# A perceiver block on one core: an entry norm, a PV product and a softmax placed elsewhere in the ramp of a hand-ordered kernel

## The reference, cut to what matters

```python
x = x + fake_quant(layernorm(x)) @ fake_quant(ctx)      # x (16,64,1024), ctx (16,1024,1024)
qkv = layernorm(x) @ Wqkv                               # 32 heads of 32, one key/value head
p = softmax(where(causal, q @ k.T * scale + alibi, -1e30))
x = x + (p @ v) @ Wo
h = layernorm(x); r = softmax(h @ gate_w.T)             # 8 experts
x = x + (h * (r @ in_scale)) @ sign(W).T * (r @ out_scale) + bias
```

## Time and profile before

| what | us |
|---|---|
| median of 3 runs | 449.78 (448.64 to 451.35) |
| the profiled execution, its own time | 451.25 |
| its span, first to last instruction | 449.5 |
| TensorE busy | 375.2 (83%) |
| VectorE busy | 310.6 (69%) |
| ScalarE busy | 259.3 (58%) |
| GpSimd busy | 97.0 (22%) |

### The profile page before, as it was taken

The page is one execution under the profiler, slowest core; times in us unless marked ns, Lnnn a source line. Parts: engine busy times, 40 slices in busy tenths (PEclk is TensorE's granted clock), DMA queues, the critical chain, the costliest instruction groups (busy, mean ns, idle before and its releaser), DMA issues.

```text
span 449.5 us, 9600 instructions
## 1 busy us (share of the span) xinstructions
PE 375.2 (83%) x3952; PEld 256.8 (57%) x3952; DVE 310.6 (69%) x586; ACT 259.3 (58%) x308; POOL 97.0 (22%) x116
## 2 busy tenths in 40 slices
PE   0445864996999979999999999998999899889565
PEld 0115834963645945596559655964588458745332
DVE  7678479884656858885888588849785975394331
ACT  4777897848495646665657575747565622241110
POOL 5210010001403404140313032312231212021202
PEclk9955996996999999999999999999999999999759
DMA  7999997699588744776477646874491010001001
GB/s 314 383 408 409 409 358 280 210 388 344 196 337 294 231 176 148 268 255 201 140 253 265 211 142 220 296 214 140 167 335 43 0 48 2 3 1 48 0 0 47
DMA packets 30097, 91.97 MB, mean 205 GB/s; under 512 B 8224, under 2 KB 8224, under 8 KB 30048
## 3 DMA queue, kind: packets, MB, share of 16 engines
q1 hardware_dynamic: 27888, 83.40, 52.3%
q10 hardware_dynamic: 2160, 7.87, 4.7%
HBM read 85.50 MB, written 4.19 MB: 200 GB/s over the span
## 4 chain that ended last, share of the span: by engine, by line
PE 60%; DVE 16%; DMA 9%; issue 6%; ACT 6%; POOL 1%; SPq 1%; POOLq 0%; DVEq 0%; ACTq 0%
PE R L1507 10%; DMA ring<-ctx 7%; PE T L1330 7%; PE R L1281 6%; PE R L1283 6%; PE R L1282 6%; PE R L1369 4%; PE R L1372 4%; PE R L1371 4%; PE C L1311 4%; ACT b L522 4%; PE T L1463 3%; DMA aT<-a 2%; DVE Pr L979 2%; DVE st L875 1%
## 5 line engine op out<-in xcount | busy, mean ns | idle before, releaser
L522 ACT ACTIVATE b<-ring,quant,qpar 128x2048 uint8<-128x2048 f32 x64 | 133.0, 2090 | 12.5 <-DMA ring<-ctx 12.0
L1369 PE MATMUL R<-T_hi,Wqkv_hi 128*128 128x128 f16 x448 | 79.3, 223 | 0.0
L1371 PE MATMUL R<-T_lo,Wqkv_hi 128*128 128x128 f16 x448 | 79.2, 222 | 0.0
L1372 PE MATMUL R<-T_hi,Wqkv_lo 128*128 128x128 f16 x448 | 79.2, 222 | 0.0
L1507 PE MATMUL R<-sgn,XS_hi 128*128 128x512 fp8e4 x128 | 49.7, 388 | 0.0
L1507 PE MATMUL R<-sgn,XS_lo 128*128 128x512 fp8e4 x128 | 49.5, 387 | 0.0
L1311 PE MATMUL C<-b,aT 128*64 128x512 f16 x256 | 36.6, 415 | 14.2 <-ACT b L522 10.1
L1369 PEld LDWEIGHTS R<-T_hi,Wqkv_hi 128*128 128x128 f16 x448 | 45.1, 101 | 0.4
L1371 PEld LDWEIGHTS R<-T_lo,Wqkv_hi 128*128 128x128 f16 x448 | 44.6, 100 | 0.1
L1372 PEld LDWEIGHTS R<-T_hi,Wqkv_lo 128*128 128x128 f16 x448 | 44.6, 100 | 0.0
L316 POOL TENSOR_TENSOR Pr<-Pr,mx 128x512 f32<-128x512 f32 x16 | 16.7, 1042 | 127.1 <-DVE mx L984 127.1
(11 more groups left out here) (143 smaller groups left out, 883.5 us busy)
## 6 DMA issues: line engine op xcount, KB each, us to landing
ring<-ctx SPq DMA_DIRECT2D x64, 1024.0 KB, 6.0
ring<-L_attn_Wo SPq DMA_DIRECT2D x4, 1024.0 KB, 7.1
ring<-L_ffn_weight SPq DMA_DIRECT2D x4, 1024.0 KB, 4.9
out<-X ACTq DMA_DIRECT2D x8, 512.0 KB, 2.6
Wo<-L_attn_Wqkv SPq DMA_DIRECT2D x7, 544.0 KB, 15.4
X<-x ACTq DMA_DIRECT2D x7, 512.0 KB, 4.1
sgn<-L_attn_Wqkv SPq DMA_DIRECT2D x1, 544.0 KB, 18.3
X<-x SPq DMA_DIRECT2D x1, 512.0 KB, 12.7
```

The costliest lines, as they stand in the source:

```text
L522: e.activation(b8[:, c % BRING, :], ring[:, slot, :], ACT.Identity, scale=qR2, bias=qZ2).then_inc(s_rf[slot], 1)
L1369: e.matmul(dst, hi, rows[0], start=k == 0 and g == 0, stop=False, skip_group_check=True)
L1371: e.matmul(dst, hi, rows[1], start=False, stop=False, skip_group_check=True)
L1372: last = e.matmul(dst, lo, rows[0], start=False, stop=k == KT - 1, skip_group_check=True)
```

## The change

It writes another order for the ramp. (1) In step 0, the last two k blocks of the second query half come after the transposition of the keys, and ScalarE and VectorE take the key parts between the two query halves. (2) In step 1, the second half of tile 0's probabilities is transposed and multiplied by v around tile 1's second norm: TensorE before and after `t1`, ScalarE and VectorE accordingly; VectorE's row normalization of tile 0 comes after v instead of before the norm. (3) Tile 1's exponentials are taken with one conversion between them, where two and one stood before; the second projection half is cut in two around a transposition; context pair 1 of tile 2 goes behind the router. (4) Tile 3's load, statistics and entry norm go from step 2 into step 1, the norm between the last `attn_rows` and `router_max`; its scratch is XL. SyncE's transposing DMA for tile 3 then stands before two loads of tile 3's context. GpSimd's list follows. The end of `step_1` also changes: `x2(ahead, 1)` before `x1(ahead)`, `context(2, 3)` after the projection, `t1(ahead)` after `ffn(ahead, 1, low)`.

```diff
 turns()
-    uses += of(1, "T10 T11") + of(0, "PT10 PT11 Ta0") + of(1, "Tk") + of(0, "Ta1")
+    uses += of(0, "PT10 PT11") + of(1, "T10 T11") + of(0, "Ta0") + of(1, "Tk") + of(0, "Ta1")
 SyncE
-                if s.is_step(2):
-                    turn_over(2)
+                if s.is_step(2, 3):
+                    turn_over(s.i)
...
-                if s.i > 2:
+                if s.i > 3:
                     turn_over(s.i)
 GpSimd, step_1
+                inv_std(0, 3)
                 inv_std(2, 0)
                 with_row_sum(2)
                 with_bias(0)
+                with_row_sum(3)
+                inv_std(2, 1)
                 inv_std(1, 2)
-                inv_std(2, 1)
 ScalarE, step_1
                 load_x(2)
+                load_x(3)
                 wo_hi(0)
+                pt_hi(s, 1, 0)
+                pt_hi(s, 1, 1)
                 wo_hi(1)
...
+                exp(ahead, 0, 0)
                 conv(2, 0)
-                conv(2, 1)
-                exp(ahead, 0, 0)
-                conv(2, 2)
                 exp(ahead, 0, 1)
...
-                conv(2, 3)
+                conv(2, 1)
...
+                conv(2, 2)
+                conv(2, 3)
+                router_exp(s)
+                ta_hi(ahead, 1)
                 conv(2, 4)
-                router_exp(s)
+                rt_copy(s)
 VectorE
-            def norm0(t, between=lambda: None):
-                if t > 1:
-                    e.wait_ge(s_Ta, (t - 1) * 2)
-                if t == 3:
-                    e.wait_ge(s_T1, 6)
+            def norm0(t, rows, between=lambda: None):
+                if rows is XL:
+                    e.wait_ge(s_T2, (t - 2) * 2)
+                else:
+                    at_least(e, s_Ta, (t - 1) * 2)
...
                 pt_lo(ahead, 0, 1)
+                stats0(3)
                 x2(s, 1)
...
                 attn_rows(ahead, 1, 1)
+                norm0(3, XL)
                 router_max(s)
 TensorE, step_0 and step_1
-                    query(s, 1, [k])
+                    if k < KT - 2:
+                        query(s, 1, [k])
                 tk(s)
+                query(s, 1, range(KT - 2, KT))
...
-                t1(s)
-                kv(s)
                 pt(s, 1, 0)
                 pt(s, 1, 1)
+                t1(s)
+                pv(s, 1, 0)
+                pv(s, 1, 1)
+                kv(s)
                 query(s, 1, low)
                 ta(s, 0)
-                pv(s, 1, 0)
-                pv(s, 1, 1)
...
                 pt(ahead, 0, 0)
+                project(s, 1, high[:2])
                 pt(ahead, 0, 1)
-                project(s, 1, high)
+                project(s, 1, high[2:])
...
                 context(2, 0, s)
-                context(2, 1)
...
                 router_t(s)
-                context(2, 2)
+                context(2, 1)
                 inscale(s, 0)
                 inscale(s, 1)
+                context(2, 2)
                 project(ahead, 0, high)
-                context(2, 3)
                 project(ahead, 1, high)
+                context(2, 3)
```

More of the change, by code:

```diff
@@ L490, in second_half @@
                     inv_std(1, s.i)
-                if s.next:
+                if s.next and not s.is_step(2):
                     inv_std(0, s.i + 1)
@@ L678, in step_0 @@
                 q_hi(s, 0)
+                k_hi(s)
                 q_hi(s, 1)
-                k_hi(s)
                 v_copy(s)
@@ L701, in step_1 @@
                 v_copy(s)
-                pt_hi(s, 1, 0)
-                pt_hi(s, 1, 1)
                 wo_hi(3)
@@ L728, in step_1 @@
                 t2_copy(s, 1)
+                conv(2, 2)
+                conv(2, 3)
+                router_exp(s)
+                ta_hi(ahead, 1)
                 conv(2, 4)
-                router_exp(s)
+                rt_copy(s)
                 conv(2, 5)
-                ta_hi(ahead, 1)
-                rt_copy(s)
+                xs_hi(s, 0)
+                xs_hi(s, 1)
                 conv(2, 6)
                 conv(2, 7)
-                xs_hi(s, 0)
-                xs_hi(s, 1)
                 conv(3, 0)
+                outscale_copy(ahead)
                 conv(3, 1)
-                outscale_copy(ahead)
             def first_half(s):
@@ L763, in second_half @@
                 f, m, b, n = s.front, s.middle, s.back, s.next
-                if n:
+                if n and not s.is_step(2):
                     load_x(s.i + 1)
@@ L889, in norm @@
                 ins_done(ins)
-            def norm0(t, between=lambda: None):
-                if t > 1:
-                    e.wait_ge(s_Ta, (t - 1) * 2)
-                if t == 3:
-                    e.wait_ge(s_T1, 6)
+            def norm0(t, rows, between=lambda: None):
[3 more added lines that the diff above has]
+                    at_least(e, s_Ta, (t - 1) * 2)
                 e.wait_ge(s_rstd[0], t + 1)
-                link(e.tensor_scalar(tok[:, :], x_in(t)[:, :], mv[0][:, 0:1], rstd[0][:, 1:2],
+                link(e.tensor_scalar(rows[:, :], x_in(t)[:, :], mv[0][:, 0:1], rstd[0][:, 1:2],
                                      ALU.subtract, ALU.mult))
@@ L903, in norm0 @@
                 at_least(e, s_aT, 16 * (t - 2))
-                link(e.tensor_scalar(aq, tok[:, :], qR1, qZ1, ALU.mult, ALU.add))
+                link(e.tensor_scalar(aq, rows[:, :], qR1, qZ1, ALU.mult, ALU.add))
                 link(e.tensor_scalar(aq, aq, 0.0, 255.0, ALU.max, ALU.min))
@@ L1121, in entry @@
                 stats0(0)
-                norm0(0)
+                norm0(0, tok)
                 stats0(1)
-                norm0(1)
+                norm0(1, tok)
                 scales_by_part()
@@ L1134, in step_0 @@
                 q_lo(s, 0)
+                k_lo(s)
                 q_lo(s, 1)
-                k_lo(s)
                 v_lo(s)
@@ L1144, in step_1 @@
                 x1(s)
-                attn_rows(s, 0, 0)
-                attn_rows(s, 0, 1)
+                pt_lo(s, 1, 0)
+                pt_lo(s, 1, 1)
                 norm1(s)
@@ L1152, in step_1 @@
                 v_lo(s)
-                pt_lo(s, 1, 0)
-                pt_lo(s, 1, 1)
-                wo_lo(2)
+                attn_rows(s, 0, 0)
+                attn_rows(s, 0, 1)
                 attn_rows(s, 1, 0)
                 attn_rows(s, 1, 1)
+                wo_lo(2)
                 ta_lo(s, 0)
@@ L1164, in step_1 @@
                 q_lo(s, 0)
-                norm0(2)
+                norm0(2, tok)
                 softmax_in(1)
@@ L1187, in step_1 @@
                 x2(ahead, 0)
+                x2(ahead, 1)
                 x1(ahead)
-                x2(ahead, 1)
                 norm1(ahead)
@@ L1224, in second_norm @@
                         norm2(s)
-                if n:
-                    norm0(s.i + 1, second_norm)
+                if n and not s.is_step(2):
+                    norm0(s.i + 1, tok, second_norm)
                 else:
@@ L1575, in step_1 @@
                 router_t(s)
-                context(2, 2)
+                context(2, 1)
                 inscale(s, 0)
                 inscale(s, 1)
+                context(2, 2)
                 project(ahead, 0, high)
+                project(ahead, 1, high)
                 context(2, 3)
-                project(ahead, 1, high)
                 outscale(ahead, 0)
@@ L1585, in step_1 @@
                 ffn(ahead, 0, high)
+                ffn(ahead, 1, low)
                 t1(ahead)
-                ffn(ahead, 1, low)
                 ffn(ahead, 1, high)
```

## The result

The changed kernel takes 446.45 us (median of 7 runs, 443.82 to 447.99), the kernel before beside it 450.25 (448.64 to 454.84): ratio 0.9895, 95% interval 0.985 to 0.9939. The interval leaves out 1, so it is faster by about 1%, inside the range of 441.8 to 448.5, and 1.25 us behind the forecast of 445.2. The profiled execution took 443.82 with a span of 442.0; it is the shortest of its seven, so its distance to the profile before, 7.43 us, is more than the distance of the medians, 3.80.

A forecast was written before the change was run, and what follows sets the result against it. TensorE, busy 83% of the span, was taken as the bound, so removed waits count: 5.45 - 1.0 - 1.2 + 1.0 + 1.8 = 6.05 us off the profiled 451.25 gives 445.2, range 441.8 to 448.5.

The forecast's parts named there:

- The likeliest case: Whole kernel: the forecast of 445.2 us, own range 443.7 to 446.7, chance 0.48.
- Tile 0's keys: Step 0: TensorE's 1.8 us wait for key parts shrinks to 1.3, worth about 0.45.
- Tile 1's norm: Tile 1's softmax starts at 96.3 instead of 97.28, gain 1.0, bound by a DMA and VectorE.
- Exponentials: Tile 1: second exponential near 102, second `x2` half at 106.7 instead of 112.14; gain at this point 5.45.
- Behind the router: Step 1 after `router_t`: context pairs 1 and 2 cost 1.0 and 1.2; output scale gives 1.0, aT 1.8.
- pair 2: Tile 2's context behind the router: TensorE waits for the sixth conversion, minus 1.2 (0 to 3).
- the output scale's 1.0: TensorE's 1.0 us wait at L1499 goes, as `x2(ahead, 1)` ends before context pair 3 does.
- The norm costs nothing: VectorE before the router: tile 3's norm takes 3.66, covered by the 3.68 us wait for the router's result.
- the integer pass: Tile 3's norm: misses GpSimd's bias add by 0.8 to 1.3; rival that they meet: 446.2, chance 0.06.
- the clock falls once more: Rival near 110 us: 6.83 us at clock 0.50 during TensorE's waits, minus 2.7, 447.9; chance 0.10.
- aT, plus 1.8: Tile 3's transposed rows: their DMA starts near 131, 20 us ahead of use, so TensorE's 1.8 us wait goes.
- Profile and median: Profiled execution, 451.25, lies 1.47 above the median of 449.78; not subtracted, else 443.7.

The follow-up runs named there:

- e10: Changed kernel with tile 3's norm back in step 2 and the third low part of Wo earlier on VectorE: 443.79 us, ratio 0.9879 to before.
- e1: Kernel before plus parts 1 and 2 only (tile 0's keys and second PV): 451.22 us, ratio 1.0002.
- e4: Changed kernel without part 4 (tile 3's load, statistics and norm back in step 2): 444.85 us, ratio 0.9851 to before.
- e2: Kernel before plus part 3 only (order of exponentials, split projection, context pairs, end of step 1): 443.95 us, ratio 0.9857.
- e8: Changed kernel without part 3, so parts 1, 2 and 4 together: 449.31 us, ratio 0.9972 to before.
- e5: The changed kernel itself, measured and profiled a second time: 446.32 us, ratio 0.9888 to before.
- e9: Changed kernel with tile 3's statistics in buffers of their own, right behind tile 2's statistics: 444.12 us, ratio 0.9863 to before.
- e7: Changed kernel without parts 1 and 2 (tile 0's parts), so parts 3 and 4 together: 447.89 us, ratio 0.992 to before.
- e6: Changed kernel with tile 3's statistics moved from ahead of `x2(s, 1)` to behind the third norm: 447.34 us, ratio 0.9918 to before.
- e12: Changed kernel with tile 3's norm back in step 2, Wo's third low part earlier and context pair 2 later: 445.11 us, ratio 0.9883.
- e11: Changed kernel with tile 3's norm back in step 2 and tile 2's context pair 2 behind the projection's first high half: 444.77 us, ratio 0.988.
- e3: Kernel before plus part 4 only (tile 3's load, statistics and norm in step 1): 449.33 us, ratio 0.9941.

## Why the prediction was right, and what in it was not

The likeliest case came: faster, by waits of TensorE in the ramp, with VectorE setting the pace. Step by step:

- **Tile 0's keys**: 0.45 expected, 0.3 seen (1.8 to 1.5). **Tile 1's norm**: softmax at 96.3 expected, 96.53 seen, bound by the signed weight's piece as said; e10 shows that bound by moving it. But this 1.0 of the sum is not seen in the time: without part 3 it turns into wait (e1), and beside part 3 parts 1 and 2 add nothing that shows (distance 99.14 in e4 with them, 99.09 in e2 without).
- **Exponentials**: 102 and 106.7 expected, 101.68 and 107.08 seen. The step that carries the gain was right to 0.4 us. e2 shows that part 3 by itself brings the gain, and e8 that the rest without it is not told apart from before. Part 3 alone even wins more distance (7.16) than the whole change (5.77, and 4.04 in e5).
- **Behind the router**: pair 2 waits 0.81 (1.2 expected), the output scale's 1.0 is gone, aT's 1.8 is gone. From `x2(s, 1)` (5.06 earlier) to tile 2's scores (5.61 earlier) 0.55 was won, 0.6 expected. That the two agree is luck: in e9, with the clock at 1.00, the same stretch wins 1.34; the price of the clock, which was not in the sum, took the rest.
- **The norm costs nothing: the step that was mis-sized.** For the four passes it was true: the router wait covers them, 3.68 became 0.38, and the integer pass missed the bias add. I put the added statistics into VectorE's path as 1.6, and 1.68 it was (e9 against the change). TensorE's waits from 104 to 111 are 0.64, 0.84 and 2.01. Their 3.49 is the 3.5 that I named for the rival, but I had put each under 1.4. They are the same 1.68 seen from TensorE: the transposition behind them starts 3.80 behind `x2(s, 1)`, in e9 3.83. What the sum had at nothing is what came with them, the clock. In all three profiles that have the new exponentials and these statistics ahead of `x2(s, 1)` (after, e5, e7) the clock falls near 110; in the other lists with the new exponentials (e2, e4, e6, e9 to e12) in none. Each of the three falls begins inside the 2.01 wait. That the wait causes the fall is not shown: in e11 TensorE waits 2.98 near 152 with no fall behind it. This is the rival "the clock falls once more", to which I gave 0.10. From tile 1's first score to tile 2's the change takes 64.26 and e9 61.79; of the 2.47 between them 1.68 stand at `x2(s, 1)`, which leaves 0.79 beside 3.4 us at 0.50. In e5, with 6.8 us at 0.50, the stretch takes 65.76, which leaves 2.29, near the 2.7 of the rival.
- **aT, plus 1.8**: true against the profile of before, but not a constant. Without the move the wait was 0.31 to 2.98 (e4 0.31, e12 0.36, e2 0.43, e10 1.21, before 1.84, e1 1.89, e11 2.98), as the DMA took 3.3 to 5.4 us. So part 4 is worth 0.6% alone (e3) and with part 3 about nothing or less (e2 and e4 against the change: the medians are 1.5 to 2.5 us lower, the intervals overlap).
- **Profile and median**: I did not subtract the 1.47 between before's profiled execution and its median. The ramp's 5.6 fits the 6.05, and the ratio's interval, 2.8 to 6.8 us of 451.25, holds it; the medians moved by 3.80. What lies between is not assigned: the executions without a profile left no trace. Of what the traces show, the ramp of e5, with the longer fall, is 1.73 longer than that of after, and the common end varies by 3.4. So the 1.25 between forecast and median is no better evidence for the sum than the steps above.

On the rule of the Trainium skill ("SBUF — State Buffer", section "Who interferes with whom"): the integer pass misses the case, as predicted. That the norm's first pass, of which the prediction said nothing, misses it too, by 0.05, is luck. e6 meets the case. There the pass that began 1.02 after GpSimd's add ended 0.55 after the end of the add, where the pass alone takes 0.80: by that rule the 1.35 left of the add are lost, and 1.10 were, so the trace agrees to 0.25. In e3, e8 and e9 the same pass begins 0.4 before the end of the add, takes 0.97, and also ends 0.55 after it.

## What to carry to other kernels

When a softmax or an exponential starves TensorE, first move the producer's own list: one conversion instead of three ahead of an exponential, with the projection cut in two around a transposition, was worth 1.4%, and the other moves added nothing to it that the times show. Once that is done another engine is full, so put added work into its real idle time (e9), not ahead of a result that TensorE awaits, where 1.7 us cost 2.5 in one profile and 4.3 in another. Judge a change of the ramp by the place where the lists become equal again, not by the end of one execution, and profile one list twice to see how much that place moves by itself (1.7 us here).

## What the runs showed of the hardware

The same end of the list, from tile 2's first score on, took 284.7 to 288.1 us in 14 profiled executions. In seven of them the clock is at 0.50 for 3.4 us, beginning 4 to 5 us behind tile 7's first score and about 1 us behind a 1.9 wait that all 14 have; from tile 7's first score to the end these take 59.2 to 59.4, the others 56.9 to 57.9. The windows of e9 and of the changed kernel, each from 0.8 behind that wait:

```profile
386.10:389.50 3.40, 3.40 (x9) 0.93 (x8) 3.37 (x7) 0.10 (x1) 1.04 (x1) 0.50 0.01 2
```

```profile
389.30:392.70 3.40, 3.13 (x15) 1.25 (x14) 3.37 (x7) 1.30 (x2) 1.04 (x1) 1.00 0.01 2
```

The one begins 9 matrix instructions at half clock, the other 15 at full. Why it falls in one and not in the other, these runs don't show. The length of a single wait doesn't settle it: behind tile 3's aT wait a fall came in e1 (1.89), and none in before (1.84) and in e11 (2.98). Nor do they show why a transposing DMA of 128 x 1024 takes 3.1 us at one time, 4.9 or 5.4 at another with loads in flight, and 10.6 (after) or 12.0 (e10) for tile 2's aT, behind context loads on the same queue.
